# First feed-forward layer: four PSUM banks for the row transposes, another order of the weight loads, and half of the expert loads issued after four gathers

## What is computed

```python
def _L0_ffn_ref(x, router_w, ..., sw1, sb1, sw2, sb2, sw3, sb3):
    xt = x.reshape(-1, DIM)                       # 1024 rows of 512
    logits = xt @ router_w + router_b             # 16 experts
    scores = softmax(logits) + router_bias
    ...                                           # 2 of 4 groups, then K = 2 experts per row
    def step(y, p):                               # one expert
        h = silu(xt @ w1 + b1) * (xt @ w2 + b2)   # 512 -> 128
        return (y + ge[:, None] * (h @ w3 + b3), None)
    z = silu(xt @ sw1 + sb1) * (xt @ sw2 + sb2) @ sw3 + sb3   # shared expert, 512 -> 256 -> 512
    return (y + z).reshape(shape)
x = x + 0.5 * _L0_ffn_ref(_layernorm(x), ...)
x = x + _L0_attn_ref(_layernorm(x), ...)
x = x + 0.5 * _L0_ffn_ref(_layernorm(x), ...)
```

## Time and profile before

| what | value |
|---|---|
| device time, median of 3 runs | 455.72 us (453.3 to 458.74) |
| the profiled execution: span from first to last instruction | 449.1 us |
| what lies between that span and the median | 6.6 us |
| PE busy | 394.0 us (88% of the span) |
| DVE, ACT, POOL busy | 270.9, 174.9, 162.9 us |
| mean granted TensorE clock | 0.992 |
| moved by DMA | 66.05 MB, mean 147 GB/s |

### The profile page before, as it was taken

One profiled execution on the slowest core, in us unless ns is written; L12 is line 12 of the kernel. 1 busy time (PEld: TensorE's weight loads), 2 busy tenths in 40 slices (PEclk: granted clock), 3 DMA queues, 4 the chain that ended last, 5 costly groups with the idle time before them and its releaser, 6 DMA issues.

```text
span 449.1 us, 8313 instructions
## 1 busy us (share of the span) xinstructions
PE 394.0 (88%) x2788; PEld 276.8 (62%) x2789; DVE 270.9 (60%) x695; ACT 174.9 (39%) x292; POOL 162.9 (36%) x230
## 2 busy tenths in 40 slices
PE   0899899999969998879979989979999879999972
PEld 0687578888647666645545555434587558888650
DVE  4579623333378954888885795666539933233357
ACT  1321246566112312166653454553441326665300
POOL 2521326665304842343432242343001054666300
PEclk9999999999999999999999999989999999999998
DMA  7999994534298569113312200010420043444278
GB/s 231 290 376 311 316 320 164 167 94 160 98 358 251 157 153 218 52 41 96 89 57 59 79 23 11 16 34 23 161 95 0 0 142 109 155 131 151 87 275 332
DMA packets 51180, 66.05 MB, mean 147 GB/s; under 512 B 8318, under 2 KB 30502, under 8 KB 51108
## 3 DMA queue, kind: packets, MB, share of 16 engines
q1 hardware_dynamic: 42780, 43.55, 30.7%
q0 software_dynamic: 6368, 19.32, 13.5%
q10 hardware_dynamic: 2000, 2.76, 2.1%
HBM read 46.32 MB, written 19.79 MB: 147 GB/s over the span
## 4 chain that ended last, share of the span: by engine, by line
PE 55%; DVE 21%; DMA 13%; SPq 4%; issue 4%; POOL 1%; ACT 1%; ACTq 0%; DVEq 0%; POOLq 0%
PE ps L1559 15%; PE ps L1566 7%; PE ps L1709 6%; PE ps L1423 5%; PE ps L1544 4%; DVE arena L1199 3%; PE ps L1685 3%; DMA turns<-in_L_ffn_sw_dram 3%; PE ps L1628 3%; DMA q_dram<-arena 3%; SPq L394 2%; PE ps L1657 2%; DMA arena<-xn_dram,arena 2%; DMA x<-_attn_hidden_states_dram 2%; PE ps L1659 2%
## 5 line engine op out<-in xcount | busy, mean ns | idle before, releaser
L1199 DVE TENSOR_REDUCE arena<-ps 128x3 f32<-128x384 f32 x128 | 68.6, 553 | 24.8 <-PE ps L1659 22.5
L1559 PE MATMUL ps<-arena,wj 128*128 128x128 f32 x608 | 74.1, 274 | 0.0
L1559 PEld LDWEIGHTS ps<-arena,wj 128*128 128x128 f32 x608 | 71.0, 192 | 1.0 <-issue 1.0
L806 ACT ACTIVATE arena<-ps 128x768 f32<-128x768 f32 x64 | 51.3, 811 | 52.0 <-PE ps L1673 51.7
L627 POOL TENSOR_SCALAR_AFFINE_SELECT arena<-arena 128x512 f32<-128x512 f32 x64 | 41.1, 642 | 78.8 <-ACT arena L806 78.4
L1096 DVE SCALAR_TENSOR_TENSOR arena<-ps,arena 128x128 f32<-128x128 f32 x38 | 13.3, 351 | 82.3 <-ACT arena L713 80.4
L1423 PE MATMUL ps<-arena,turns 128*128 128x256 f32 x256 | 57.6, 381 | 0.5 <-DMA turns<-in_L_ffn_sw_dram 0.5
L1423 PEld LDWEIGHTS ps<-arena,turns 128*128 128x128 f32 x256 | 48.1, 190 | 8.9 <-issue 2.1
L554 POOL DMA_INDIRECT arena<-xn_dram,arena x34 | 33.3, 979 | 50.7 <-DVE arena L1036 25.2
L559 POOL DMA_INDIRECT y_dram<-arena x38 | 38.5, 1012 | 34.4 <-DVE arena L1103 25.4
L1657 PE MATMUL ps<-cb 128*128 128x256 bf16 x128 | 35.4, 276 | 12.0 <-DVE arena L1199 11.4
(11 more groups left out here) (198 smaller groups left out, 601.4 us busy)
## 6 DMA issues: line engine op xcount, KB each, us to landing
arena<-y_dram SPq DMA_DIRECT2D x16, 512.0 KB, 7.7
arena<-q_dram SPq DMA_DIRECT2D x36, 128.0 KB, 2.6
xn_dram<-arena SPq DMA_DIRECT2D x16, 256.0 KB, 6.3
w<-in_L_ffn_ew_dram SPq DMA_DIRECT2D x4, 1024.0 KB, 10.5
q_dram<-arena SPq DMA_DIRECT2D x16, 192.0 KB, 2.5
x<-_attn_hidden_states_dram SPq DMA_DIRECT2D x4, 512.0 KB, 6.4
out_dram<-x SPq DMA_DIRECT2D x8, 256.0 KB, 5.4
arena<-arena SPq DMA_DIRECT2D x30, 64.0 KB
```

What stands on the lines that cost most here:

```text
L806: act.activation(pr[:, n % 2, pair, :], ps[:, bank:bank + 2, :].rearrange("p a b -> p (a b)")[:, 0:768], ACT.Exp).then_inc(sem("exp"), 1)
L1199: dve.tensor_reduce(m3[:, h:h + 1, :], ps[:, bank, 0:3 * P].rearrange("p (n k) -> p n k", n=3), AX_X, ALU.max).then_inc(sem("s_max"), 1)
L1559: ins = pe.matmul(o, wj[:, par, c, n * INTER:(n + 1) * INTER], xgT[:, par, c, :], start=(c == 0), stop=(c == KC - 1))
```

## The change

It touches the first FFN only.

- The turns of the first FFN go round four banks, `TURN_BANKS` (PS_XT, PS_XT + 1, PS_HT, PS_Y). Turn t waits for copy t - 4 in place of t - 2. DVE's two copies count on a semaphore of their own, `xnT_dve`, and no copy waits for another.
- ACT issues only sw1 and sw2. sw3 (with a semaphore `sw3_in` of its own) and w1 and w2 of group 0 are issued by SP, behind the eight stores of `xn`. The first `shared_up` waits for sw1 and sw2 alone; the first `shared_down` waits for sw3.
- Ahead of group 2 (`HELD = 8`) SP waits until the gathers of jobs 0 to 3 have landed.

```diff
@@ build
+HELD = 8
...
+        TURN_BANKS = (PS_XT, PS_XT + 1, PS_HT, PS_Y)
@@ ffn_sp
+                nc.sync.dma_start(sw3s[:], sw3.rearrange("(c p) d -> p c d", p=P)).then_inc(sem("sw3_in"), 16)
                 for e in range(0, E, EG):
+                    if e == HELD:
+                        for j in range(4):
+                            nc.sync.wait_ge(sem(f"xg0_{j}"), 16)
                     for part in range(2):
-                        if e > 0:
-                            experts_in(nc.sync, e, part)
+                        experts_in(nc.sync, e, part)
@@ block.sync
-            experts_in(sp, 0, 1)
             ffn_sp(0)
@@ xn_bank, xnT_copy
-            return (PS_XT if f == 0 else PS_S) + t % 2
+            return TURN_BANKS[t % len(TURN_BANKS)] if f == 0 else PS_S + t % 2
...
-            if f == 0 and t > DVE_TURNED[0]:
-                nc.scalar.wait_ge(sem("xnT"), t)
@@ block.scalar
-            act.dma_start(sw3s[:], sw3.rearrange("(c p) d -> p c d", p=P)).then_inc(sem("sw_in"), 16)
-            experts_in(act, 0, 0)
@@ ffn_dve
-                    dve.wait_ge(sem("xnT"), t)
-                    dve.tensor_copy(..., ps[:, xn_bank(0, t), :]).then_inc(sem("xnT"), 1)
+                    dve.tensor_copy(..., ps[:, xn_bank(0, t), :]).then_inc(sem("xnT_dve"), 1)
@@ xn_turn
-            if t >= 2:
-                pe.wait_ge(sem("xnT"), NT * f + t - 1)
+            back = len(TURN_BANKS) if f == 0 else 2
+            if t >= back:
+                pe.wait_ge(sem("xnT"), xnT_by_act(f) + t - back + 1)
@@ ffn_pe
             if f == 0:
-                pe.wait_ge(sem("sw_in"), 48)
+                pe.wait_ge(sem("sw_in"), 32)
...
-                if t == 2 and f == 1:
-                    pe.wait_ge(sem("wo_in"), 48)
+                if t == 2:
+                    pe.wait_ge(sem("sw3_in") if f == 0 else sem("wo_in"), 16 if f == 0 else 48)
```

More of the change, by code:

```diff
@@ L651, in xn_bank, with xnT_by_act @@
         def xn_bank(f, t):
-            return (PS_XT if f == 0 else PS_S) + t % 2
+            return TURN_BANKS[t % len(TURN_BANKS)] if f == 0 else PS_S + t % 2
+        def xnT_by_act(f):
+            return NT * f - (len(DVE_TURNED) if f >= 1 else 0)
         def xnT_copy(f, t):
             nc.scalar.wait_ge(sem("xt"), NT * f + t + 1)
-            if f == 0 and t > DVE_TURNED[0]:
-                nc.scalar.wait_ge(sem("xnT"), t)
             nc.scalar.copy(xnT[:, t].rearrange("p c q -> p (c q)"), ps[:, xn_bank(f, t), :]).then_inc(sem("xnT"), 1)
@@ L912, in ffn_dve @@
                     dve.wait_ge(sem("xt"), t + 1)
-                    dve.wait_ge(sem("xnT"), t)
-                    dve.tensor_copy(xnT[:, t].rearrange("p c q -> p (c q)"), ps[:, xn_bank(0, t), :]).then_inc(sem("xnT"), 1)
+                    dve.tensor_copy(xnT[:, t].rearrange("p c q -> p (c q)"), ps[:, xn_bank(0, t), :]).then_inc(sem("xnT_dve"), 1)
             else:
@@ L1436, in ffn_pe @@
                 shared_up(1, 1, (1,))
-            pe.wait_ge(sem("xnT"), NT * f + NT)
+            pe.wait_ge(sem("xnT"), xnT_by_act(f + 1))
+            if f == 0:
+                pe.wait_ge(sem("xnT_dve"), len(DVE_TURNED))
             if f == 0:
```

## The result

The changed kernel took 471.25 us (median of 4 runs, 467.9 to 471.77), the kernel before 454.51 us beside it (its three runs of above and a fourth): ratio 1.037, 95% interval 1.030 to 1.044. It is slower by 16.7 us; forecast were 9.0 us, and 471.25 lies outside the range.

The account below looks back on a forecast made before the run. PE was taken as the bound, running the first FFN's jobs without a gap. down(3) 7.4 us later, with 2.8 us of front gain inside, plus 1.6 us of clock gave +9.0: 455.7 to 464.7 us, range 459.5 to 469.

Parts of the forecast that it names:

- That is all that this load may be late by: ACT's wait for all groups after weights_copy(4): loads in at 66.1, ACT past the wait at 69.9, slack 3.8 us.
- B: Rival, chance 0.11: the refill runs at 401 GB/s, down(3) is 1.8 us later, the kernel takes 459.1 us.
- C: Rival, chance 0.03: ACT's wait does not bind and only the front counts, 2.8 us gained, 452.9 us.
- D: Rival, chance 0.11: engines stay full at the gathers, gather 3 takes 7.1 us, lands at 59.6; 468.3 us.
- the sum for down(3): First FFN: gather 3 landed 56.0, plus 2 and 21.3, ACT on at 79.3; down(3) at 80.4, 7.4 us later.
- 21.3 us: Time for groups 2 and 3 (6.3 MB) to load after the hold; bounds 15.7 and 23 us.
- 2 us: Delay of the held loads' first bytes on idle engines after the release; bounds 1 and 3 us.
- with the handover: From ACT going on at 79.3 to down(3) at 80.4, including 1.0 us from silu to down.
- 2.2 us earlier: Front: first shared_up starts at 21.2 in place of 23.45, gathers likewise earlier; bounds 0.5 and 2.6 us.
- 0.93 each: Front: cost of one turn; with four banks turn 7 starts when tile 7 is there, logits 1.75 us earlier.
- The gathers: On idle engines a gather takes 3.5 us in place of 7.1, removing PE's 0.6 us wait; bounds 3 and 7.1.
- the clock: PE's idle stretch ahead of down(3) lowers its clock to half level, adding 1.6 us to the work behind it.

Follow-up runs that it names:

- e1_no_hold: The changed kernel without SP's wait for the four gathers; banks and new load order stay: 453.49 us, ratio 0.9992 to the kernel before.
- e2_hold_alone: The kernel before with one edit, SP waiting for the four gathers ahead of the third group: 472.42 us, ratio 1.039.
- e3_wait_later: The changed kernel with ACT's wait for all groups moved four jobs later, behind weights_copy(8): 460.54 us, ratio 1.016 to the kernel before.
- e5_two_gathers: The changed kernel with SP waiting for two gathers in place of four: 468.05 us, ratio 1.035 to the kernel before.
- e7_warm_front: The changed kernel without the hold, plus five fp32 products, never read, on PE ahead of the first turn: 452.10 us, ratio 0.9986 to before.
- e4_pe_busy: The changed kernel with 62 extra bf16 products, never read, on PE ahead of turn(5): 467.24 us, ratio 1.029 to the kernel before.

## Why the prediction was right in kind and wrong in size

**The main mechanism held.** "That is all that this load may be late by" was the right question, and the held loads were late by far more. e1_no_hold and e2_hold_alone leave the hold with the whole loss, e3_wait_later shows that its price sits mostly at ACT's early wait, e5_two_gathers that down(3) follows the release one for one. The rivals B and C (a fast refill, a wait that does not bind) did not come; nor did D: the gathers ran on free engines (a DMA share of 0.00 from 48 to 50 us).

**The failed step is the sum for down(3):** 80.4 forecast, 86.77 measured, 6.4 us short, from three terms of 4.0, 0.9 and 1.3 us.

- *The refill, "21.3 us" and "2 us" for the start: 23.3, measured 27.3 us* (27.3 and 27.4 in e2_hold_alone and e5_two_gathers). This is the largest miss, 4.0 us. The windows split the 27.3 us: some 1.8 us from the issue until the engines are full (near 59.2), 24 us at full share, and 1.5 us from the fall of the share, near 83.3, to 84.76, where the last load is counted as landed. So the 2 us for the start were right, and the end was missing: the lag between the fall of the share and the landing. It was missing twice. I had begun the two groups' time before the change at a landing (44.3) and ended it at 66.1, where the DMA share falls from full. By the same lag, as an estimate, they took 23.3 us from landing to landing, not 21.8, and ACT's slack was 2.3 us, not 3.8. The rest of the 4.0 us is the step from 21.8 down to 21.3 and a slightly slower transfer. The load of x had shown both ends: 3.2 us beyond its bytes, and I took 2. My upper bounds (3 and 23) add up to 26.
- *ACT after its wait, "with the handover": 0.1, measured 1.0 us.* Between the landing at 84.76 and silu(3) at 85.77 lie the loop's entry and the loads of expert numbers into registers. Before, they ran in the shadow of PE.
- *The front, "2.2 us earlier": 0.9 us at the first shared_up, 1.0 us at the gathers.* The release came at 57.3, not 56.0, the other 0.1 us by the slightly longer gather. The step "0.93 each", with turn 7 starting when tile 7 is there, was wrong: six turns follow each other at 0.86 us (5.13 us in all), so PE is behind DVE's rows, and the banks remove only 0.4 us. e7_warm_front shows the cause: PE at half speed (421 ns for a product in place of 273), with a granted clock of 1.00 in the record.

**The gathers** (3.5 us forecast, 3.63 and 3.45 measured), silu to down (1.0 us both) and **the clock** (1.6 us forecast, 1.76 from down(3) to down(4), 1.7 by e4_pe_busy) were right. That the clock's term fits so well is in part luck: the same stretch lost 2.6 us in e2_hold_alone and e5_two_gathers. With 13.7 + 1.8 = 15.5 us the place is accounted for, and the last down is 15.5 us late; the medians differ by 16.7 us. The 1.2 us between them are within the spread of either kernel and stay open.

**The range** had the bounds of each term but not their sum: they were combined toward the middle, and ACT's entry had no bound at all.

## What to carry to other kernels

Before holding a transfer back, look for every wait on it, also those placed early for convenience, and count the slack from landing to wait; a hold of H us there costs about H less that slack, one for one, plus what a start from idle queues costs against loads that follow one another (4 us here, 27.3 against an estimated 23.3) and the clock of an idle TensorE (1.7 to 2.6 us). A prefetch that runs beside the router's bookkeeping is cheap; the same bytes beside the jobs slow their gathers and scatters, and a result buffer that waits for its scatter then delays the next gather in the same queue. Here the gathers were 3.5 us faster and PE had been waiting 0.6 us for them.

## What was not expected of the hardware

- In the front of every trace but one the turns begin at half speed while the record says 1.00. Two turns took 1.94 us there, as two turns of the attention did in a stretch of the changed kernel with a recorded 0.50 (the first two rows below, a timeline's and a window's), and 1.04 us after 6 us of work (e7_warm_front). The moment at which they speed up differs between executions: the 24 products of six turns took 5.38, 5.13, 4.63 and 4.37 us in four traces with the same order of PE. Only a duration shows this; the recorded clock does not.

```profile
148.37 1.94 PE L1623 MATMUL ps<-cf,arena 128*128 128x128 f32 x8 [2.52 <-DVE arena L1174]
...
148.37:150.31 1.94, 1.94 (x9) 0.50 1.04 392
...
132.87 1.07 PE L1617 MATMUL ps<-cf,arena 128*128 128x128 f32 x8 [2.52 <-DVE arena L1171]
```

The Trainium skill ("TensorE: Matmul & The Clock Gate", section "Part 1: The HAM clock gate (the "warmup" mystery)") calls the throttled state the default; the durations agree, the recorded clock of the front does not.
- The short pauses of PE in the attention lower the clock in some executions and not in others: behind the same pause of 2.52 us the two turns took 1.94 us in the changed kernel's trace (the first row above) and 1.07 us in that of the kernel before (the last). Runs of the kernel before had mean clocks from 0.975 (454.9 us) to 0.993 (450.0 us). One trace with 0.992 is a best case, and a difference of two spans can be off by some 5 us (448.0 to 453.2 us for one kernel).
- The DMA share falls about 1.5 us before the semaphore of the last load is counted. For a wait, the landing counts.
